# Moving one head's softmax scaling from VectorE to GpSimd, and one PSUM copy ahead of a normalisation, in a fused attention and expert kernel

## The chip, the cores and the metric

The kernel runs on one core of one Trainium2 chip. The metric is device time in microseconds (us) of one execution of the whole program, as the median of several runs. Five engines work from queues of their own: PE (TensorE, matmuls; its weight loads are shown as PEld), DVE (VectorE), ACT (ScalarE), POOL (GpSimd) and SP, which only issues DMAs here. They meet at semaphores.

## The reference, cut to what matters

```python
h = concat([patches(x) @ W.T + b, txt], axis=1)             # 8 sequences of 36 + 512 tokens, width 192
h = h + attn(layernorm(h)); h = h + experts(layernorm(h))

def attn(x):                                                # 3 heads of 64
    scores = einsum('blhe,bmhe->bhlm', q, k) / 8
    scores = scores * where(m >= l, gamma_h ** (m - l), 0)  # zeroed, not masked out
    w = softmax(scores, axis=-1)
    o = einsum('bhlm,bmhe->blhe', w, v)
    o = (o - mean(o)) / sqrt(var(o) + eps)                  # per sequence and head
    return (o.reshape(B, L, D) * gn_weight + gn_bias) @ Wo.T

def experts(x):                                             # 16 experts, 8 chosen per token
    return sum(comb[:, e] * (gelu(x @ w1[e]) @ w2[e]) for e in range(16))
```

A key before the query has the score zero, so it still counts in the softmax: every row of probabilities has a stored part on and above the diagonal and one common value for all keys below it, whose sums over the values come in through 4 extra columns.

## The kernel before, in words

The work has two parts. The first 315 us or so are attention, one sequence b at a time, eight in all (b = 0, 1, a hardware loop over 2 to 6, and 7). Each of the functions called `body` gives one engine its order for one sequence. The second part is the experts: 24 weight tiles for each of 9 token tiles, PE-dense, which the change does not touch.

A sequence's 548 queries are cut into five blocks I = 0 to 4 (four of 128, one of 36). The stored scores of block I have 580, 452, 324, 196 and 68 columns, 1620 in all. One head of one sequence runs like this:

- PE makes the scores in PSUM (`scores`). DVE multiplies them by the decay and takes row maxima (`apply_decay`, the custom instruction of L912), then negates the maxima (`nm`, L918: one column after block 0, four columns at the end).
- ACT takes the exponentials with row sums (`exps`, L598), block by block, into `pr0` (heads 0 and 2) or `pr1` (head 1), and the exponential of the zero score (L595).
- DVE makes the denominators: three small instructions (L925, L927, L929). It then scales the five blocks of `pr` by them (L935). Together these are `normalise`. It starts with a wait for all five exponentials of that head (`exp_done`), and ends with the semaphore `probs_ready`. For head 2 ACT does two of the five blocks (L565).
- PE transposes `pr` in four groups of 4, 4, 4 and 3 blocks (`probs_transpose`, L1316). It waits for the scaling before the first. ACT copies each group from PSUM to `pt` (`pt_copy`, L516). PE multiplies by the values (`attend`), six products, of which the first three need the groups 0 and 1, the fourth the group 2, the last two the group 3. Each shows as two rows per product in the trace.

Between these lie other pieces. On PE: `values` makes the value rows after head 1's scores; its last block waits until DVE has done all decays of head 1. `gn_sums` is a 4-column product on DVE's statistics of the previous sequence's output (`gn_partial`, L943 to L950). On DVE: `norm_stats` for the next sequence in front of head 1's decay, `gn_partial` between the two `normalise` calls, and `gn_variance` (L954 to L960) behind the second. On POOL, one sequence at a time: `rstd_of` (power, L425, and two small ones, L426 and L428), `halve_w1` (two casts L447 and two subtractions L450 of 384 columns), `gn_coefficients` (L459 to L465), which ends with `y_coeff`, and a small copy (L434). On ACT: `v_copy` between head 1's exponentials, and `y_round` and `y_whole` (L626), which scale the previous sequence's output and wait for `y_coeff`.

In the last sequence (b = 7) ACT also normalises the first expert tile (`second_norm(0)`) ahead of head 0's exponentials, and DVE splits that tile's transposes (`x2_rest`) behind head 1's decay; PE's first router products (`logits(0, 2)`, L1178 with `rw`) wait for these.

Of the kernel before, what the change touches and what calls it, by code (L numbers as in the profile page):

```python
# [38 lines left out]
NT = -(-L // P)  # L39
# [58 lines left out]
def nth(b, per, k):  # L98

    return b * per + k  # L100


def early_fusion(nc, patches, txt, tok_w, tok_b, gammas, gn_w, gn_b, attn_w, w1, w2, out):
# [9 lines left out]
    with ctx:  # L113
# [112 lines left out]
        s_done, decayed, nm_ready = sem("s_done"), sem("decayed"), sem("nm_ready")  # L226
        exp_done, den_ready, probs_ready = sem("exp_done"), sem("den_ready"), sem("probs_ready")
        probs_scaled = sem("probs_scaled")
        pt_done, pt_copied = sem("pt_done"), sem("pt_copied")
# [168 lines left out]
        def _(pool):  # L398
# [57 lines left out]
            def gn_coefficients(t):  # L456
# [8 lines left out]
                pool.tensor_tensor(gshift[:, :], gnb[:, :], gsub[:, :], ALU.subtract).then_inc(y_coeff, 1)  # L465

            def second_rstd(t):
                rstd_of(t, ln2_var, rstdb, mvb, vepsb, nmrb, ln2_rstd, SEG)
# [17 lines left out]
            def body(b, tail, later, more):  # L486
                if not more:
                    second_rstd(0)
                    second_twice(0)
                if more:  # L490
                    rstd_of(b + 1, ln1_var, rstd, mv, veps, nmr, ln1_rstd)
                halve_w1(b)
                if tail:
                    gn_coefficients(b - 1)
                if more:
                    twice(ln1_normed, nth(b, 1, 1), xn, xn_ready)
# [15 lines left out]
        def _(sc_eng):  # L512
# [141 lines left out]
            def body(b, tail, later, more):  # L654
# [27 lines left out]
                else:  # L682
                    logits_exp(0)
                if tail:
                    y_round(t, 0)
                pt_copy(b, 1, (0, 1))
                if tail:
                    y_whole(t, 0)
                    y_round(t, 1)
# [101 lines left out]
        def _(dve):  # L791
# [127 lines left out]

            def normalise(b, hh):  # L920

# [7 lines left out]
                last = dve.reciprocal(inv_den[s][:, :], den[s][:, :])  # L929
                if hh == 2:  # L930
                    last.then_inc(den_ready, 1)
                dve.drain()
# [104 lines left out]
            def body(b, tail, later, more):  # L1037
# [10 lines left out]
                if more:  # L1048
                    norm_stats(b + 1, st6, mv, veps, ln1_var)
                apply_decay(b, 1)  # L1050
                if not more:
                    x2_rest(0, 0, 4)
                    x2_rest(0, 1, 5)
                normalise(b, 0)
                if tail:
# [120 lines left out]
        def _(pe):  # L1176
# [133 lines left out]
            def probs_transpose(b, hh, groups=(0, 1, 2, 3)):  # L1310
# [7 lines left out]
                for g in groups:  # L1318
                    if g == 0:

                        pe.wait_ge(probs_ready, nth(b, H, hh + 1))
                        if hh == 2:
# [270 lines left out]
```

## Time and profile before

| | |
|---|---|
| median of 3 runs | 849.03 us (848.9 to 854.23) |
| the profiled execution | 850.09 us |
| its span in the trace | 848.3 us |
| mean granted TensorE clock | 0.983 of full speed |
| PE busy | 805.3 us, 95% of the span |
| DVE busy | 558.7 us, 66% |
| ACT busy | 508.2 us, 60% |
| POOL busy | 101.1 us, 12% |

Times in the rows are counted from the start of the span. A row in order of time gives its start, the time from its start to the end of its last instruction, the engine, the line in the kernel, the operation, output and inputs, and how many instructions it merges; brackets hold the time for which the engine had stood idle and who released it. Back-to-back instructions of an engine overlap a little, so a row can start shortly before the one ahead of it ends. Each iteration of the loop over sequences takes about 36 us and shows the same pattern; the rows are mostly of b = 2, from about 101 to 137 us.

### The profile page before, as it was taken

What the parts mean: (1) busy time and instruction counts of PE and PEld (TensorE: products, weight loads), DVE (VectorE), ACT (ScalarE), POOL (GpSimd) and SP (SyncE); (2) the same over time, 40 slices, a digit from 0 to 9 for tenths busy, and PEclk for the clock granted to TensorE, in tenths of its full rate; (3) what the DMA queues carried; (4) which work ended last, traced back from release to release, by engine and by line L of the source; (5) the groups of instructions that cost most, each with busy time, mean ns of one, the idle gap of its engine ahead of it and who ended that gap; (6) DMA issues with size and microseconds to landing.
All of it is one profiled execution on the core that took longest, in us unless ns stands there. A gap on an engine that the chain in (4) does not pass through costs nothing.

```text
span 848.3 us, 13687 instructions
## 1 busy us (share of the span) xinstructions
PE 805.3 (95%) x4336; PEld 678.4 (80%) x4336; DVE 558.7 (66%) x1559; ACT 508.2 (60%) x1134; POOL 101.1 (12%) x187
## 2 busy tenths in 40 slices
PE   6799999999999998799999999999999999999997
PEld 2677878797787876677888888888888888888886
DVE  5667677677767777565666666666666566666654
ACT  1367867778777774465555645556555556465443
POOL 2022020220202208300101001001010010000000
PEclk9689999999999999999999999999999999999999
DMA  7400010101103027213422324134133241241420
GB/s 221 152 19 17 5 40 0 38 0 38 38 0 93 1 60 208 79 50 93 120 63 71 106 62 133 41 85 123 53 96 91 68 128 47 80 96 61 113 56 18
DMA packets 44376, 60.77 MB, mean 72 GB/s; under 512 B 4018, under 2 KB 37762, under 8 KB 44322
## 3 DMA queue, kind: packets, MB, share of 16 engines
q1 hardware_dynamic: 44322, 60.10, 25.5%
q8 instruction: 27, 0.44, 0.2%
q14 instruction: 27, 0.22, 0.1%
HBM read 52.04 MB, written 8.05 MB: 71 GB/s over the span
## 4 chain that ended last, share of the span: by engine, by line
PE 61%; issue 26%; POOL 6%; POOLq 3%; DVE 2%; ACT 2%; DVEq 0%; ACTq 0%
PE ps L1178 58%; POOL w_lo L450 2%; POOLq L427 1%; POOL w_lo L482 1%; PE ps L1378 1%; POOLq L460 1%; POOLq L481 1%; POOL w_r L480 0%; PE ps L1316 0%; PE ps L1487 0%; ACT pt L516 0%; PE ps L1488 0%; DVE sc L912 0%; POOLq L448 0%; PE ps L1397 0%
## 5 line engine op out<-in xcount | busy, mean ns | idle before, releaser
L1089 DVE TENSOR_TENSOR act<-act,gate 128x480 f32<-128x480 f32 (+1 forms) x216 | 145.1, 672 | 120.0 <-ACT act L714 118.7
L1178 PE MATMUL ps<-x,w_hi 128*128 128x480 f32 (+1 forms) x648 | 217.4, 390 | 0.0
L714 ACT ACTIVATE act<-ps 128x480 f32<-128x480 f32 (+1 forms) x216 | 124.0, 574 | 125.9 <-PE ps L1178 125.7
L1178 PE MATMUL ps<-x,w_lo 128*128 128x480 f32 (+1 forms) x432 | 165.6, 383 | 0.0
L867 DVE TENSOR_TENSOR act_lo<-act,act_hi 128x480 fp32r<-128x480 f32 (+1 forms) x216 | 144.3, 668 | 0.1
L1178 PEld LDWEIGHTS ps<-x,w_hi 128*128 128x128 f32 x648 | 122.5, 189 | 19.8
L516 ACT ACTIVATE act_hi<-act 128x480 fp32r<-128x480 f32 (+1 forms) x216 | 130.8, 605 | 7.9 <-DVE act L1089 7.9
L1178 PEld LDWEIGHTS ps<-x,w_lo 128*128 128x128 f32 x432 | 81.8, 189 | 13.3
L1178 PE MATMUL ps<-act_hi,w_hi 128*128 128x480 f32 (+1 forms) x216 | 83.9, 388 | 6.6 <-DVE act_lo L867 6.6
L1178 PE MATMUL ps<-act_lo,w_hi 128*128 128x480 f32 (+1 forms) x216 | 83.8, 388 | 0.0
L1178 PE MATMUL ps<-act_lo,w_r 128*128 128x480 f32 (+1 forms) x216 | 83.0, 384 | 0.0
L1178 PE MATMUL ps<-act_hi,w_lo 128*128 128x480 f32 (+1 forms) x216 | 82.8, 384 | 0.0
L1178 PE MATMUL ps<-pt,v 68*128 68x512 f32 (+5 forms) x288 | 82.4, 436 | 0.0
L1178 PE MATMUL ps<-act_hi,w_r 128*128 128x480 f32 (+1 forms) x216 | 82.3, 381 | 0.0
L1178 PEld LDWEIGHTS ps<-pt,v 128*128 128x128 f32 (+1 forms) x288 | 49.0, 190 | 31.1 <-issue 21.6
L598 ACT ACTIVATE pr<-sc,nm 128x580 f32<-128x580 f32 (+4 forms) x120 | 66.8, 559 | 10.7 <-DVE nm L918 10.7
L912 DVE CUSTOM_DVE_ANT_0 sc<-ps,decay 128x548 f32<-128x548 f32 (+4 forms) x120 | 49.7, 458 | 35.5 <-PE ps L1178 33.3
L516 ACT ACTIVATE pt<-ps 128x384 f32<-128x384 f32 (+3 forms) x120 | 48.4, 466 | 23.8 <-PE ps L1316 23.6
L1316 PE MATMUL ps<-ident,pr 128*128 128x128 f32 (+1 forms) x360 | 47.2, 276 | 11.6 <-DVE pr L935 9.1
L425 POOL TENSOR_TENSOR rstdb<-vepsb,neg_half 128x4 f32<-128x4 f32 x9 | 12.2, 1353 | 364.9 <-DVE vepsb L989 364.9
L1178 PEld LDWEIGHTS ps<-act_hi,w_hi 128*128 128x128 f32 x216 | 40.5, 187 | 16.4 <-DVE act_lo L867 9.9
L1316 PEld LDWEIGHTS ps<-ident,pr 128*128 128x128 f32 (+1 forms) x360 | 39.1, 132 | 15.7 <-DVE pr L935 10.9
(173 smaller groups left out, 1318.1 us busy)
## 6 DMA issues: line engine op xcount, KB each, us to landing
gate<-comb_dram SPq DMA_DIRECT2D x112, 240.0 KB, 3.3
gate<-comb_dram SPq DMA_DIRECT2D x32, 256.0 KB, 3.7
w_raw<-w SPq DMA_DIRECT2D x16, 384.0 KB, 3.9
h_dram<-h SPq DMA_DIRECT2D x8, 384.0 KB
res<-h_dram SPq DMA_DIRECT2D x7, 360.0 KB, 4.5
out<-res SPq DMA_DIRECT2D x7, 360.0 KB, 3.2
h<-txt SPq DMA_DIRECT2D x3, 672.0 KB
decay_rows<-drow SPq DMA_DIRECT2D x1, 1014.0 KB, 8.0
```

The lines of the kernel that those rows point to most:

```text
L425: pool.tensor_tensor(rs[:, :], ve[:, :], neg_half[:, 0:n], ALU.pow)
L427: pool.drain()
L450: last = pool.tensor_tensor(w1_lo[:, c, cols], w1_raw[:, c, :], w1_hi[:, c, cols], ALU.subtract)
L460: pool.drain()
L516: return a.activation(dst, src, ACT.Copy)
L598: last = a.activation(pr[s][:r, cols], sc[s][:r, cols], ACT.Exp, bias=nm[s][:r, I:I + 1], accum_out=row_sum[s][:r, I:I + 1])
L714: a.activation(act[j % 3][:, 0:n], ps[:, up_bank(j), 0:n], ACT.Gelu_apprx_tanh).then_inc(gelu_done, 1)
L867: return dve.tensor_tensor(dst, src, hi, ALU.subtract)
L912: dve.tensor_tensor_reduce(out=dst, in0=src, in1=tab, scale=1.0 / 8, scalar=0.0 if I else NEG, op0=ALU.mult, op1=ALU.max, accum_out=mx[s][ ...
L1089: dve.tensor_tensor(act[j % 3][:, 0:n], act[j % 3][:, 0:n], gate[e % 4][:, 0:n], ALU.mult).then_inc(gated, 1)
L1178: return pe.matmul(dst, w, x, start=start, stop=stop)
L1316: return pe.transpose(dst, pr[s][:, at:at + n], ident[:, :])
```

## The change

For head 0 the scaling is taken from DVE. DVE makes head 0's denominators ahead of head 1's decay (`denominators(b, 0)`) and signals `first_den`; POOL waits for it, scales the five blocks of `pr0` (`normalise_first`), and signals `first_probs`, for which PE waits in place of `probs_ready`. On POOL this is ahead of `rstd_of` and `halve_w1`; in b = 7 behind `second_twice`. On ACT the copies of head 1's first two groups of transposes go ahead of `y_round`.

```diff
+            def normalise_first(b):
+
+                pool.wait_ge(first_den, nth(b, 1, 1))
+                apart(pool, "pool")
+                for I in range(NT):
+                    t = pr[0][:rows(I), OFF[I]:OFF[I] + WIDTH[I]]
+                    last = pool.tensor_scalar(t, t, inv_den[0][:rows(I), I:I + 1], None, ALU.mult)
+                last.then_inc(first_probs, 1)
...
                 if not more:
                     second_rstd(0)
                     second_twice(0)
+                normalise_first(b)
                 if more:
                     rstd_of(b + 1, ln1_var, rstd, mv, veps, nmr, ln1_rstd)
                 halve_w1(b)
...
+                pt_copy(b, 1, (0, 1))
                 if tail:
                     y_round(t, 0)
-                pt_copy(b, 1, (0, 1))
-                if tail:
                     y_whole(t, 0)
                     y_round(t, 1)
                 pt_copy(b, 1, (2, 3))
...
-            def normalise(b, hh):
+            def denominators(b, hh):
...
                 last = dve.reciprocal(inv_den[s][:, :], den[s][:, :])
-                if hh == 2:
-                    last.then_inc(den_ready, 1)
+                if hh != 1:
+                    last.then_inc((first_den, None, den_ready)[hh], 1)
+
+            def normalise(b, hh):
+                s = hh % 2
+                denominators(b, hh)
                 dve.drain()
...
                 if more:
                     norm_stats(b + 1, st6, mv, veps, ln1_var)
+                denominators(b, 0)
                 apply_decay(b, 1)
                 if not more:
                     x2_rest(0, 0, 4)
                     x2_rest(0, 1, 5)
-                normalise(b, 0)
                 if tail:
                     gn_partial(t)
                 normalise(b, 1)
...
-                        pe.wait_ge(probs_ready, nth(b, H, hh + 1))
+                        if hh:
+                            pe.wait_ge(probs_ready, nth(b, 2, hh))
+                        else:
+                            pe.wait_ge(first_probs, nth(b, 1, 1))
```

DVE's queue in the loop body before, from the end of `norm_stats` over head 1's decay to the statistics of the previous sequence's output (`st`, `mv`, `veps`: the next sequence's statistics; `sc`, `mx`, `nm`: scores, maxima, negated maxima; `gst`: the output's statistics):

```order
L828 TENSOR_SCALAR veps<-mv 128x5
...
L912 ISA sc,mx<-ps,decay 128x548
...
L918 TENSOR_SCALAR nm<-mx 128x4
L923 ISA
L925 TENSOR_TENSOR den<-zero_score,lower_count 128x5
L927 TENSOR_TENSOR den<-den,row_sum 128x5
L929 RECIPROCAL inv_den<-den 128x5
L935 TENSOR_SCALAR pr<-pr,inv_den 128x580
...
L943 BN_STATS gst<-ot 128x6 x2
```

There the denominators stand behind the decay. The same stretch of DVE's queue in the changed kernel:

```order
L838 TENSOR_SCALAR veps<-mv 128x5
L933 ISA
L935 TENSOR_TENSOR den<-zero_score,lower_count 128x5
L937 TENSOR_TENSOR den<-den,row_sum 128x5
L939 RECIPROCAL inv_den<-den 128x5
...
L922 ISA sc,mx<-ps,decay 128x548
...
L928 TENSOR_SCALAR nm<-mx 128x4
L955 ISA
L957 BN_STATS gst<-ot 128x6 x2
```

The three denominator instructions moved in front of the decay, and the five scalings are gone from the queue.

POOL's queue in the loop body of the changed kernel, from its start to the split of w1 (before, the body began with the `rstd` row):

```order
L474 TENSOR_SCALAR pr<-pr,inv_den 128x580
L474 TENSOR_SCALAR pr<-pr,inv_den 128x452
L474 TENSOR_SCALAR pr<-pr,inv_den 128x324
L474 TENSOR_SCALAR pr<-pr,inv_den 128x196
L474 TENSOR_SCALAR pr<-pr,inv_den 36x68
...
L426 TENSOR_TENSOR rstd<-veps,neg_half 128x5
...
L448 COPY w_hi<-w_raw 128x384
...
L451 TENSOR_TENSOR w_lo<-w_raw,w_hi 128x384
```

Everything that POOL did for a sequence is now queued behind the five scalings and behind their wait.

ACT's queue in the loop body before, behind the normalisation of the next sequence (`xn`; `y` and `ot` with `gshift` are `y_round` and `y_whole`, `pt` the copies of transposes):

```order
L546 ACTIVATE xn<-h,nmr,rstd 36x192
L626 ACTIVATE y<-ot,gshift,gscale 128x548
...
L516 ACTIVATE pt<-ps 68x512
...
L516 ACTIVATE pt<-ps 128x384
L626 ACTIVATE ot<-ot,gshift,gscale 128x548
```

Here `y_round` stands first. The same stretch of ACT's queue in the changed kernel:

```order
L557 ACTIVATE xn<-h,nmr,rstd 36x192
...
L527 ACTIVATE pt<-ps 68x512
...
L527 ACTIVATE pt<-ps 128x384
L637 ACTIVATE y<-ot,gshift,gscale 128x548
L637 ACTIVATE ot<-ot,gshift,gscale 128x548
```

The three copies of the groups 0 and 1 changed places with the first of the four instructions that wait for `y_coeff`.

## Rows read from the trace of the kernel before

**Rows 1.** The page: busy us, share of the span, instructions.

```profile
PE 805.3 (95%) x4336; PEld 678.4 (80%) x4336; DVE 558.7 (66%) x1559; ACT 508.2 (60%) x1134; POOL 101.1 (12%) x187
```

**Rows 2.** Waits of PE: who was waited for, us in total, times, longest.

```profile
PE ps L1316 <- DVE pr L935: 9.1, 7, 1.4
...
PE ps L1178 <- DVE gmv L950: 3.3, 7, 0.5
```

**Rows 3.** PE in order of time, b = 0 and then b = 2.

```profile
50.34 1.83 PE L1316 MATMUL ps<-ident,pr 128*68 128x128 f32 x15 [1.37 <-DVE pr L935]
...
120.64 1.83 PE L1316 MATMUL ps<-ident,pr 128*68 128x128 f32 x15 [1.37 <-DVE pr L935]
122.95 0.36 PE L1178 MATMUL ps<-gmv,head_mean 128*128 128x4 f32 x2 [0.47 <-DVE gmv L950]
123.31 3.50 PE L1178 MATMUL ps<-pt,v 68*128 68x512 f32 x12
126.64 1.04 PE L1316 MATMUL ps<-ident,pr 128*68 128x128 f32 x8
...
129.91 3.40 PE L1178 MATMUL ps<-pt,v 68*128 68x512 f32 x12
```

**Rows 4.** DVE in order of time, b = 2.

```profile
114.95 0.73 DVE L912 CUSTOM_DVE_ANT_0 sc<-ps,decay 128x548 f32<-128x548 f32 x1 [1.63 <-PE ps L1178]
...
117.48 0.89 DVE L918 TENSOR_SCALAR nm<-mx 128x4 f32<-128x4 f32 x1
118.28 0.15 DVE L925 TENSOR_TENSOR den<-zero_score,lower_count 128x5 f32<-128x5 f32 x1
...
119.02 1.57 DVE L935 TENSOR_SCALAR pr<-pr,inv_den 128x580 f32<-128x580 f32 x5
...
123.50 1.57 DVE L935 TENSOR_SCALAR pr<-pr,inv_den 128x580 f32<-128x580 f32 x5
```

**Rows 5.** ACT in order of time, b = 2.

```profile
113.89 0.19 ACT L598 ACTIVATION_READ_ACCUMULATOR pr<-sc,nm 36x1 f32 x1
...
117.53 0.66 ACT L516 ACTIVATE v<-ps 128x128 f32<-128x128 f32 x2 [0.69 <-PE ps L1178]
118.40 0.21 ACT L595 ACTIVATE zero_score<-nm 128x5 f32<-128x5 f32 x1 [0.21 <-DVE nm L918]
...
121.31 1.06 ACT L516 ACTIVATE pt<-ps 68x512 f32<-68x512 f32 x3 [0.20 <-PE ps L1316]
...
127.68 0.84 ACT L626 ACTIVATE y<-ot,gshift,gscale 128x548 fp32r<-128x548 f32 x1 [1.94 <-POOL gshift L465]
128.43 1.04 ACT L516 ACTIVATE pt<-ps 68x512 f32<-68x512 f32 x3
...
130.83 0.96 ACT L516 ACTIVATE pt<-ps 128x512 f32<-128x512 f32 x2
```

**Rows 6.** Groups on POOL, shapes kept apart: busy us, mean ns of one; idle before.

```profile
L450 POOL TENSOR_TENSOR w_lo<-w_raw,w_hi 128x384 f32 x10 | 9.9, 1014 | 1.1 <-issue 1.1
L425 POOL TENSOR_TENSOR rstd<-veps,neg_half 128x5 f32<-128x5 f32 x8 | 9.4, 1181 | 162.9 <-DVE veps L828 162.9
...
L447 POOL CAST w_hi<-w_raw 128x384 f32 x10 | 4.8, 506 | 0.4
```

**Rows 7.** POOL in order of time, b = 2.

```profile
116.35 1.98 POOL L450 TENSOR_TENSOR w_lo<-w_raw,w_hi 128x384 f32 x2 [0.23 <-issue]
```

**Rows 8.** DVE in order of time, b = 7.

```profile
294.69 0.73 DVE L912 CUSTOM_DVE_ANT_0 sc<-ps,decay 128x548 f32<-128x548 f32 x1 [2.68 <-PE ps L1178]
...
298.66 0.17 DVE L925 TENSOR_TENSOR den<-zero_score,lower_count 128x5 f32<-128x5 f32 x1
```

**Rows 9.** ACT in order of time, b = 7: the end of head 0's exponentials.

```profile
295.52 0.19 ACT L598 ACTIVATION_READ_ACCUMULATOR pr<-sc,nm 36x1 f32 x1
```

**Rows 10.** PE in order of time, b = 7: router products, and head 1's third group.

```profile
299.66 1.41 PE L1178 MATMUL ps<-rw,x 128*128 128x32 f32 x12
...
309.93 1.01 PE L1316 MATMUL ps<-ident,pr 128*128 128x128 f32 x7 [0.62 <-ACT pt L516]
```

More of the change, by code:

```diff
@@ L227, in early_fusion @@
         exp_done, den_ready, probs_ready = sem("exp_done"), sem("den_ready"), sem("probs_ready")
+        first_den, first_probs = sem("first_den"), sem("first_probs")
         probs_scaled = sem("probs_scaled")
```

## The prediction, made before the changed kernel ran

> **What bounds the kernel now.** I read the page first: PE is busy for 95% of the span [rows 1], so only PE's gaps are to be had. The view of PE's waits names them. Two kinds repeat once per sequence: 9.1 us in 7 waits of the head transposes (L1316) for DVE's scaled `pr`, and 3.3 us in 7 waits for DVE's `gmv` [rows 2]. Then the engines in order of time, for one sequence, b = 2, whose pattern repeats.
>
> PE would begin head 0's transposes at 120.64 - 1.37 = 119.27, right behind the value rows, and begins at 120.64 [rows 3]. DVE's five scalings run from 119.02 to 120.59 [rows 4] and PE starts 0.05 us later; that is the hand-off I use below. They come so late only because of DVE's order: head 0's exponentials were over at 113.89 + 0.19 = 114.08 [rows 5], and the whole decay of head 1, 114.95 to 118.3, stood in between [rows 4]. The second wait, 0.47 us, is the same lateness passed on: DVE reaches the output's statistics behind the scalings. PE starts `gn_sums` at 122.95 and the first product with the values at 123.31 [rows 3].
>
> **The denominators in front of the decay.** From the first small instruction to the first scaling DVE takes 119.02 - 118.28 = 0.74 us [rows 4]. Started 0.05 us behind the exponentials, they run from 114.13 to 114.87. DVE stood idle for 1.63 us before 114.95, waiting for PE's scores [rows 4], so they fill a hole. Head 1's decay starts 0 to 0.4 us late (the 0.4 if a semaphore between the small ones stalls). What is queued behind is the decay and its `nm`, for which ACT waits; ACT's second exponential of head 1 stands behind a value copy that waits for PE until 117.53 [rows 5], which hides that much. No cost in the loop.
>
> **The scaling on POOL.** No row shows POOL's `tensor_scalar` with a column of factors. The bounds: a cast of 384 columns takes 506 ns, a subtraction of two inputs 1014 ns [rows 6]. For 1620 columns, 4.22 times as much, that is 2.13 or 4.28 us. I take 2.13 us as the nearer row: the product streams one tensor, like the cast. POOL starts at 114.9 and ends at 117.05, or 119.2 by the other row. Both are before 119.27, so PE's 1.37 us goes either way in the loop. Gone from DVE are 1.57 + 0.74 us between the decay and the statistics, so `gmv` comes some 2 us earlier and the 0.47 us goes too. PE's own floor for the first product with the values is then 123.31 - 1.37 - 0.47 = 121.47.
>
> **What is late next: ACT.** The product also needs the copies of groups 0 and 1. They stand at 121.31 behind a run of exponentials and value copies that began at 118.40, with only 0.20 us of waiting in it [rows 5]. So the copies start 118.40 to 121.31 less 0.20 = 2.71 us behind that start, take 1.06, and hand over in 0.05: 3.82 us in all. Can the start at 118.40 move? ACT waited there for `nm`, a 4-column instruction that took 0.89 us on DVE [rows 4] and ended at 118.37, just as POOL's subtractions ended, 116.35 + 1.98 = 118.33 [rows 7]. I read this as DVE held by POOL. If POOL is between long operations at 117.5 in the changed kernel, ACT starts when the value copies let it, 117.53 + 0.66 less an overlap of 0.1 = 118.1, and the product at 121.9: 1.4 us gained. If POOL holds `nm` as before, it starts at 118.4 and the product at 122.2: 1.1 us gained. With POOL's products over at 117.05, next in its queue is the power (1181 ns for 5 columns [rows 6], hardly any data), so the first is possible. I take the middle, 1.25 us, and keep both ends.
>
> The page "GPSIMD Engine Reference" of the Trainium skill, section "Key points", says that GpSimd shares its SBUF interfaces with VectorE, in contention with VectorE's instructions in a 2-port mode or with two SBUF inputs. The 0.89 us agree. By that rule alone a POOL product still running at 117.5 would hold `nm`, and the gain would be the 1.1 us.
>
> **Does the gain survive to the next sequence?** Three places behind it.
> - Head 1's scalings on DVE began at 123.50, 1.13 us behind the end of the copies (121.31 + 1.06). Now: copies end at 121.9, scalings 123.0 to 124.6. PE wants them at 126.64 - 1.4 = 125.2 [rows 3, 4]. Margin 0.6.
> - `y_coeff`: ACT's `y` began at 127.68, 2.61 us behind the end of head 1's scalings (125.07); now 127.2. Before, 127.68 to 130.83 held three `y` instructions and the copies of groups 0 and 1 (about 0.93 us as spaced), so three `y` take 2.22 us. With the copies ahead of them the group 2 copy starts at 127.2 + 2.2 = 129.4 and is done near 129.9. PE begins head 1's products at 129.91 - 1.4 = 128.5 and needs group 2 after 932 of their 1828 columns, 1.73 us of the 3.40 [rows 3, 5]: 130.2. Margin 0.3. In the old order the first copies would start at 127.2 + 0.75 and PE's third group would wait for them about 0.8 us; this is what the ACT edit is for, it gains nothing by itself in the loop.
> - POOL's queue: the power and two small ones, the casts and the subtractions now start at 117.05 and take some 4.9 us (1.8 + 1.0 + 2.0 and gaps), to about 122. The subtractions end before head 1's denominators at 122.3. Margin 0.3. The next sequence's `rstd` is wanted by ACT only at about 123.
>
> **The eight sequences.** b = 2 to 6: 5 x 1.25 = 6.25 us. b = 1: its wait for `pr` is 9.1 - 6 x 1.36 = 0.9 to 1.0 us, the shortest of the seven [rows 2]; I take 1.0. b = 0: there is no `gmv` wait and, at the start, no hole in DVE's time, so I let the 0.74 us of denominators count against the 1.37 us [rows 3]: 0.7 (bounds 0 and 1.37). b = 7: there head 0's exponentials end only at 295.52 + 0.19 = 295.71 [rows 9], a microsecond after head 1's decay began at 294.69 [rows 8]. DVE now waits for them: decay at 295.71 + 0.05 + 0.74 = 296.5, 1.8 us late. From the decay's start to the end of the two `x2_rest` DVE takes 298.66 - 294.69 = 3.97 us [rows 8], so they are done at 300.4 and PE's router products start there instead of at 299.66 [rows 10]: 0.8 us lost. The `gmv` wait (0.47) vanishes behind it, so some 0.35 is left at the first product; and head 1's third group, which waited 0.62 us for ACT's copy [rows 10], has it earlier by the ACT edit. I put b = 7 at 0, between -0.5 (gain) and +0.8.
>
> Sum: 6.25 + 1.0 + 0.7 + 0 = 7.95, say 8.0 us. The expert part is untouched and shifts as a whole. Profiled execution: 850.09 - 8.0 = 842.1. The median of the runs shown lies 1.06 us under it, so the forecast is 849.03 - 8.0 = **841.0 us**. With both ends of every term it goes from 5 x 1.1 + 0.9 + 0 - 0.8 = 5.6 to 5 x 1.4 + 1.0 + 1.4 + 0.5 = 9.9: 839.1 to 843.4.
>
> **Rivals.**
> *POOL is slow and in the way (about 847).* If the scaling runs at the subtraction's rate, POOL is done with it at 119.2 and with the split of w1 near 124.1, right through DVE's head-1 denominators and scalings (123.0 to 124.6). By the 0.89 us row each of these can be held for up to one POOL instruction of 1.0 us. One microsecond there passes to `y_coeff` and to PE's third group, whose margin is 0.3; 0.3 us per sequence is left, 2 us in all. For it: the same collision is in the trace. Against it: one input tensor, not two. The page "Perfetto Trace Analysis" of the Trainium skill, section "Optimizing Scalar/DVE Operations", says just this, that moving work between VectorE and GpSimd might not help because they share an SBUF port; by it nothing much is gained.
>
> *ACT does keep up (about 837).* If the copies were no limit, PE would start at its floor: 1.84 us for each of b = 2 to 6, 1.5 for b = 1, 1.37 for b = 0: 12.1 us. Against it stands the full ACT run of rows 5; it would need ACT to start 0.4 us before its value rows are there.
>
> *Slower: POOL's products become the wait (about 858).* Before, the scaled head 0 was there at 120.59; POOL, starting at 114.9, is later than that if it needs over 5.7 us, 3.5 ns a column. Each microsecond above costs PE one in every sequence, and in b = 7 as well. At 7 us, 4.3 ns a column, 1.3 x 7 = 9.1 us are added to 849.03. For it: no row shows the operation. Against it: its slowest neighbour needs 2.6 ns a column with two inputs.
>
> **How the numbers follow.** Forecast 0.61, slow POOL 0.23, ACT keeps up 0.10, POOL the wait 0.06. A measurement of this kernel can tell about 1% from no change, 8.5 us, so 840.5 is the border. About half of the forecast's band lies below it: 0.30, with the 0.10 of the second rival 0.40 faster. Slower by that much needs the last rival at nearly its full price: 0.05. The rest, 0.55, is within 1%. The range, 838.5 to 847.5, holds the forecast's band and most of the first rival's.
>
> **What would show it.** Right: PE's waits for `pr` and `gmv` in head 0 gone, and in their place one of 0.4 to 0.8 us per sequence in front of the products with the values, released by ACT's `pt`; POOL's five scalings near 2.1 us from first to last; the `nm` of head 1 short again; in b = 7 DVE's decay 1.8 us behind its old place relative to PE's scores, and a PE wait for `x2_rest`. Wrong: a wait of L1330 for POOL in the loop; `nm` or head 1's scalings stretched by POOL; a PE wait for `pt` in front of head 1's third or fifth product.

## The result, and the profile after

| | before | changed |
|---|---|---|
| median of 20 runs each | 850.92 us | 856.57 us |
| lowest and highest | 848.62, 855.54 us | 853.12, 858.27 us |
| ratio, with its 95% interval | | 1.0045, 1.0028 to 1.0061 |
| the profiled execution, its span | 850.09, 848.3 us | 857.33, 855.6 us |

The change makes the kernel slower, by the ratio above 0.45%. The forecast was 841.0 us with a range of 838.5 to 847.5, so it had the wrong sign. Each kernel's times fall in two groups (848.6 to 850.3 and 851.5 to 855.5 us before; 853.1 to 854.9 and 856.5 to 858.3 us after), and group by group the medians rose by 4.5 and 3.4 us. The profiled executions differ by more, 7.2 us.

The page of the changed kernel shows where work went: POOL has 43.5 us more than in [rows 1], DVE only 3.3 us less, though head 0's five scalings, 1.57 us a sequence [rows 4], have left it.

```profile
PE 808.4 (94%) x4336; PEld 679.5 (79%) x4336; DVE 555.4 (65%) x1519; ACT 508.4 (59%) x1134; POOL 144.6 (17%) x227
```

The waits of PE in the changed kernel: who was waited for, us in total, times, longest.

```profile
PE ps L1330 <- POOL pr L474: 9.4, 7, 2.4
...
PE ps L1330 <- DVE pr L949: 5.1, 6, 0.9
PE ps L1192 <- ACT pt L527: 2.0, 6, 0.3
PE ps L1192 <- DVE mx L922: 1.9, 1, 1.9
```

The 9.1 us for DVE's `pr` of [rows 2] have become 9.4 us for POOL's, and the 3.3 us for `gmv` are gone. Two new kinds came: the scaling of head 1, and ACT's copies, six times each.

POOL's groups, shapes kept apart: busy us, mean ns of one; idle before.

```profile
L474 POOL TENSOR_SCALAR pr<-pr,inv_den 128x580 f32<-128x580 f32 x8 | 13.9, 1744 | 159.2 <-DVE inv_den L939 159.2
...
L474 POOL TENSOR_SCALAR pr<-pr,inv_den 128x452 f32<-128x452 f32 x8 | 11.3, 1415 | 0.0
...
L474 POOL TENSOR_SCALAR pr<-pr,inv_den 128x324 f32<-128x324 f32 x8 | 8.7, 1094 | 0.0
L474 POOL TENSOR_SCALAR pr<-pr,inv_den 128x196 f32<-128x196 f32 x8 | 6.2, 772 | 0.0
...
L474 POOL TENSOR_SCALAR pr<-pr,inv_den 36x68 f32<-36x68 f32 x8 | 3.6, 445 | 0.0
```

A column costs (1744 - 445) / (580 - 68) = 2.54 ns, and each instruction about 0.27 us besides: 5.4 us for the five (5.38 from first to last in the row below), 2.5 times what I took (2.13) and 26% over the bound that I called the upper one (4.28).

Now one sequence of the changed kernel, b = 2, in order of time. PE:

```profile
125.13 1.83 PE L1330 MATMUL ps<-ident,pr 128*68 128x128 f32 x15 [1.17 <-POOL pr L474]
126.80 0.28 PE L1192 MATMUL ps<-gmv,head_mean 128*128 128x4 f32 x2
126.94 3.48 PE L1192 MATMUL ps<-pt,v 68*128 68x512 f32 x12
131.26 1.04 PE L1330 MATMUL ps<-ident,pr 128*68 128x128 f32 x8 [0.83 <-DVE pr L949]
...
133.54 0.98 PE L1330 MATMUL ps<-ident,pr 128*128 128x128 f32 x7
134.36 1.89 PE L1192 MATMUL ps<-pt,v 68*128 68x512 f32 x6
136.58 1.67 PE L1192 MATMUL ps<-pt,v 128*128 128x512 f32 x5 [0.33 <-ACT pt L527]
```

POOL, over the same time:

```profile
119.70 5.38 POOL L474 TENSOR_SCALAR pr<-pr,inv_den 128x580 f32<-128x580 f32 x5 [21.92 <-DVE inv_den L939]
125.04 1.19 POOL L426 TENSOR_TENSOR rstd<-veps,neg_half 128x5 f32<-128x5 f32 x1
...
126.83 0.96 POOL L448 CAST w_hi<-w_raw 128x384 f32 x2
128.00 2.17 POOL L451 TENSOR_TENSOR w_lo<-w_raw,w_hi 128x384 f32 x2 [0.21 <-issue]
131.98 0.70 POOL L460 TENSOR_TENSOR grstd<-gvar,neg_half 128x2 f32<-128x2 f32 x1 [1.81 <-DVE gvar L974]
```

And DVE:

```profile
119.67 0.73 DVE L922 CUSTOM_DVE_ANT_0 sc<-ps,decay 128x548 f32<-128x548 f32 x1 [0.18 <-PE ps L1192]
...
122.19 0.17 DVE L928 TENSOR_SCALAR nm<-mx 128x4 f32<-128x4 f32 x1
...
124.23 0.16 DVE L962 TENSOR_TENSOR gtmp<-gmv 128x2 f32<-128x2 f32 x1
...
127.45 0.35 DVE L937 TENSOR_TENSOR den<-den,row_sum 128x5 f32<-128x5 f32 x1
...
128.14 2.97 DVE L949 TENSOR_SCALAR pr<-pr,inv_den 128x580 f32<-128x580 f32 x5
```

Three things are to be read here. POOL ends head 0's scaling at 119.70 + 5.38 = 125.08, PE begins 0.05 us later and had waited 1.17 us: POOL has taken DVE's place in [rows 3], almost at the old price. Secondly, everything on POOL came late behind it, and its subtractions, 128.00 to 130.17, now lie upon head 1's scalings on DVE: five instructions that took 1.57 us before [rows 4] take 2.97 us, and PE waits 0.83 us for them. Thirdly, `y` on ACT and the copies behind it slip too, and the last products wait 0.33 us. The last row of POOL says why `y` is late: POOL stood idle for 1.81 us before `grstd`, the first step to `y_coeff`, until DVE had made `gvar` behind its stretched scalings. It was the held DVE that made `y` late, not the length of POOL's queue.

To count the loss I use marks: the first transposes that PE makes of each sequence, those of the normalised input `xn` (not those of `pr`). For b = 2 this is, in the kernel before,

```profile
97.19 1.26 PE L1216 MATMUL ps<-ident,xn 128*128 128x128 f32 x10
```

and in the changed one

```profile
101.88 1.25 PE L1230 MATMUL ps<-ident,xn 128*128 128x128 f32 x10
```

From one mark to the next it is 35.95 us in the loop before and 36.31 us after (five sequences, +1.8 us); b = 1 has 35.32 and 35.58 (+0.26); b = 0 has 35.25 and 39.75 (+4.5); from b = 7's mark to the transposes of `xn` for the expert tile behind it +0.75. That is 7.3 us, the difference of the spans. These spans are of one execution each, and most of the 4.5 us of b = 0 goes with the place of a low clock and not with the new order, as the end of the next section shows. Against the forecast (8.0 us less) 8.05 us are missing in the loop, 1.3 in b = 1, 5.2 in b = 0 and 0.75 in b = 7.

### The profile page after: what moved, and what is told of

Read it like the earlier page. It is cut to its first block, busy times and chain, and to the rows that moved or that the text cites. A ratio compares the mean times of both kernels' runs of the same rounds, so it can differ in the third digit from the quotient of the medians.

```text
span 855.6 us, 13676 instructions
## 1 busy us (share of the span) xinstructions
PE 808.4 (94%) x4336; PEld 679.5 (79%) x4336; DVE 555.4 (65%) x1519; ACT 508.4 (59%) x1134; POOL 144.6 (17%) x227
## 3 DMA queue, kind: packets, MB, share of 16 engines
q1 hardware_dynamic: 44322, 60.10, 25.1%
HBM read 52.04 MB, written 8.05 MB: 70 GB/s over the span
## 4 chain that ended last, share of the span: by engine, by line
PE 73%; POOL 9%; issue 6%; ACT 5%; POOLq 5%; DVE 2%; DVEq 0%; ACTq 0%
PE ps L1192 67%; POOL pr L474 3%; PE ps L1330 3%; ACT pr L609 2%; POOLq L428 2%; POOL w_lo L451 2%; POOL w_lo L492 1%; PE ps L1230 1%; ACT pt L527 1%; POOL rstd L426 1%; PE ps L1395 1%; ACT y L637 1%; POOLq L449 1%; POOLq L461 1%; POOLq L491 1%
## 5 line engine op out<-in xcount | busy, mean ns | idle before, releaser
L1192 PE MATMUL ps<-pt,v 68*128 68x512 f32 (+5 forms) x288 | 86.7, 449 | 2.0 <-ACT pt L527 2.0
L474 POOL TENSOR_SCALAR pr<-pr,inv_den 128x580 f32<-128x580 f32 (+4 forms) x40 | 43.0, 1094 | 159.2 <-DVE inv_den L939 159.2
L1330 PE MATMUL ps<-ident,pr 128*128 128x128 f32 (+1 forms) x360 | 50.0, 287 | 15.4 <-POOL pr L474 9.4
L1330 PEld LDWEIGHTS ps<-ident,pr 128*128 128x128 f32 (+1 forms) x360 | 41.3, 138 | 19.3 <-POOL pr L474 11.4
```

What stands on the lines that cost most here:

```text
L474: last = pool.tensor_scalar(t, t, inv_den[0][:rows(I), I:I + 1], None, ALU.mult)
L1192: return pe.matmul(dst, w, x, start=start, stop=stop)
L1330: return pe.transpose(dst, pr[s][:, at:at + n], ident[:, :])
```

## The experiments

My theory after the result: POOL's scaling runs at 2.54 ns a column, and this one wrong size does it all, by PE's wait for it and by what it pushes behind it on POOL. The rivals: that the denominators in front of the decay cost something, that ACT's new order does, or that the forecast of the rest (gain 1.25 us, then ACT the limit) was wrong too. The first four kernels take the change apart. All kernels of this section were run once, except the three for which a median of four is given; one kernel's total varies by some 4 us from run to run, so the argument rests on the rows and on the distances from mark to mark.

**Without ACT's edit.**

```diff
+                if tail:
+                    y_round(t, 0)
                 pt_copy(b, 1, (0, 1))
                 if tail:
-                    y_round(t, 0)
                     y_whole(t, 0)
```

> The changed kernel with ACT's old order. The first copies of head 1 stand behind y_round again, whose coefficients now come about 1 us after the transposes they copy. Theory (the ACT edit is needed because POOL's queue is late): PE's third group of head 1 waits 1 to 1.6 us and the loop period of 36.31 us rises to 37.3 to 37.9, the total by 7 to 10 us. Rival (the ACT edit does nothing where the bound is POOL's scaling): period stays within 0.1 of 36.31.

Measured 862.84 us (before, on the same chip, 849.18), and 37.3 us from mark to mark in the loop, except for b = 4 with 39.0, where PE's clock was granted at half from 209 to 212 us, behind such a wait for ACT. PE in order of time, b = 2, of this kernel:

```profile
122.34 1.83 PE L1331 MATMUL ps<-ident,pr 128*68 128x128 f32 x15 [1.16 <-POOL pr L474]
...
128.46 1.04 PE L1331 MATMUL ps<-ident,pr 128*68 128x128 f32 x8 [0.83 <-DVE pr L950]
...
132.31 1.01 PE L1331 MATMUL ps<-ident,pr 128*128 128x128 f32 x7 [1.40 <-ACT pt L527]
```

A third wait joins the other two: ACT stands in front of `y`, late with `y_coeff`, and head 1's third group waits 1.40 us for the copies behind it. So the ACT edit is not what costs; with the late POOL it saves 1.0 us a sequence.

**ACT's edit alone**, in the kernel before.

```diff
-                if tail:
-                    y_round(t, 0)
                 pt_copy(b, 1, (0, 1))
                 if tail:
+                    y_round(t, 0)
                     y_whole(t, 0)
```

> The kernel before with the ACT edit alone. PE has no wait for copies in the loop, so the period stays at 35.96 us within 0.1; the waits of 0.37 (b = 1) and 0.62 us (b = 7) in front of head 1's third group go. Total 0.5 to 1.5 us under before. Rival (the copies now delay y and with it the next statistics): period above 36.1.

Measured 848.60 us, and in the loop 35.66 us from mark to mark instead of 35.95. That is 0.29 us a sequence which the theory had at nothing. (The total met the expectation only because b = 0 took 37.24 us instead of 35.25, by its clock; see below.) The place shows by distances: from head 1's first transposes to its third group it is 2.57 us in the kernel before (b = 3 to 6) and 2.29 us here. PE was losing 0.28 us there all along, which the move of ACT's copies took back, and no idle bracket in [rows 3] says so.

**The denominators early, alone**: DVE still scales, behind the decay.

```diff
+                denominators(b, 0)
                 apply_decay(b, 1)
...
-                normalise(b, 0)
+                scale(b, 0)
```

> The kernel before with head 0's denominators in front of head 1's decay, the scaling left on DVE behind it. Theory (the move fills a hole of DVE): scaling starts 0.65 us earlier, PE's wait for pr falls from 1.37 to about 0.7 us and the period from 35.96 to 35.2 to 35.4; in b = 7 some 0.5 to 1 us are lost. Total 2 to 4 us under before. Rival (waiting for the exponentials holds the decay up in the loop too): period 35.9 or more.

Measured 853.19 us, more and not less than before, yet in the loop 35.59 to 35.64 us from mark to mark, 0.35 less than before. PE's wait for `pr` falls from 1.37 to 0.66 us, and 0.52 us of ACT's `pt` appears in front of head 1's third group, where this kernel has the old ACT order. So in the loop the early denominators cost nothing, as I had said. The loss is in b = 0, which takes 39.56 us (4.3 more than before) and is looked at below, and behind b = 7's mark, from where the rest takes 1.3 us more.

**POOL scales only the last block** (68 of 1620 columns), the rest of the change as it is. Four blocks stay unscaled, so the output is wrong, and the kernel serves only to measure.

```diff
-                for I in range(NT):
+                for I in range(NT - 1, NT):
```

> The changed kernel with POOL scaling only the smallest of head 0's five blocks; four blocks of head 0's probabilities stay unscaled. This stands for a POOL that is fast enough. Theory (everything lost is POOL's slow scaling and what it pushes behind it): PE's waits for pr and gmv are gone, a wait for ACT's copies of 0.4 to 0.8 us takes their place, as forecast, and the period is 34.5 to 34.9 us. If ACT keeps up: 34.1. Rival (the loss lies in the denominators' place or in the queue of POOL whatever its length): period 35.5 or more.

Measured 841.86 us (before 849.18). PE in order of time, b = 2:

```profile
119.87 1.80 PE L1330 MATMUL ps<-ident,pr 128*68 128x128 f32 x15
...
122.56 3.50 PE L1192 MATMUL ps<-pt,v 68*128 68x512 f32 x12 [0.68 <-ACT pt L527]
...
125.90 1.04 PE L1330 MATMUL ps<-ident,pr 128*68 128x128 f32 x8
...
128.19 0.98 PE L1330 MATMUL ps<-ident,pr 128*128 128x128 f32 x7
```

This is the kernel that I had forecast: no wait for `pr` or `gmv`, in their place 0.68 us for ACT's copies, and the first product with the values 1.35 us earlier after the mark than before (24.62 instead of 25.97, b = 3 to 6). With the hidden 0.28 us a sequence is 1.63 us shorter, 34.32, which is less than the 34.5 to 34.9 that I expected. For the loop the rivals fall. Against this kernel the changed one loses 1.98 us a sequence, and the marks split them: 0.43 to the first product (POOL late), 0.98 more to head 1's first transposes (DVE held), 0.57 behind its last products (`y` late).

The next kernels ask which part of the 1.98 us is the place in POOL's queue, and which the scaling itself.

**The split of w1 last on POOL.** Nothing on POOL is made faster.

```diff
                 normalise_first(b)
                 if more:
                     rstd_of(b + 1, ln1_var, rstd, mv, veps, nmr, ln1_rstd)
-                halve_w1(b)
                 if tail:
                     gn_coefficients(b - 1)
                 if more:
                     twice(ln1_normed, nth(b, 1, 1), xn, xn_ready)
+                halve_w1(b)
```

> The changed kernel with POOL's split of w1 moved from in front of gn_coefficients to the end of POOL's body. Theory (of the 1.98 us that the period of 36.31 lies above that of the one-block kernel, 34.32, 0.43 is POOL's late scaling and 1.55 is POOL's w1 subtractions holding DVE's head-1 denominators and scalings, passed on to y and PE): head 1's five scalings on DVE are 1.57 us again instead of 2.97, PE's waits of 0.83 for pr and 0.33 for pt go, the period is 34.7 to 35.0. Rival (DVE is late because it waits for ACT and POOL's scaling, not for the w1 split): period 36.0 or more.

Measured 847.66 us, which by itself says little: before, seven runs on the same chip gave a median of 853.6 and went from 848.18 to 854.3. PE, then DVE, in order of time, b = 2:

```profile
123.34 1.83 PE L1330 MATMUL ps<-ident,pr 128*68 128x128 f32 x15 [1.17 <-POOL pr L474]
...
128.46 1.04 PE L1330 MATMUL ps<-ident,pr 128*68 128x128 f32 x8
```

```profile
126.17 1.57 DVE L949 TENSOR_SCALAR pr<-pr,inv_den 128x580 f32<-128x580 f32 x5
```

The wait for POOL is the same 1.17 us, but DVE's scalings are back at 1.57 us, and from mark to mark it is 34.74 us, 1.57 less than in the changed kernel. So the collision with the subtractions, and the late `y` that comes of it, were worth 1.57 us, POOL's lateness by itself 0.4. The larger loss was the place of work that nothing waits for. That POOL's subtractions held DVE's scalings is shown by this: neither was altered, they were only moved apart.

**Two blocks on POOL** (1032 of 1620 columns), three on DVE behind the decay, w1's split where the change has it.

```diff
-                for I in range(NT):
+                for I in range(2):
...
+                scale(b, 0)
                 if tail:
                     gn_partial(t)
```

> The changed kernel with POOL scaling only the blocks 0 and 1 of head 0 (1032 of 1620 columns) and DVE the three small ones behind head 1's decay; the queue order of POOL is the changed kernel's. Everything is computed. Theory: POOL is done 3.1 us after first_den, before PE wants it, and the w1 split ends 2.2 us earlier, near DVE's head-1 denominators: period 34.4 to 35.2, total 7 to 12 us under the changed kernel. Rival (any product on POOL in this place costs more than it saves): period 35.96 or more.

Measured 844.53 us, 35.15 us from mark to mark. No wait for `pr` is left, but 0.39 us for `gmv` and 0.39 us for ACT's copies in front of the last products. A smaller load on POOL clears part of the way, yet `y` is still late.

**Both together, and b = 0 and b = 7 in the old order**: two blocks on POOL for b = 1 to 6, w1's split last, and in the first and last sequence the denominators and all five scalings on DVE behind the decay.

```diff
-                normalise_first(b)
+                if not isinstance(b, int) or b == 1:
+                    normalise_first(b)
...
-                denominators(b, 0)
+                early = not isinstance(b, int) or b == 1
+                if early:
+                    denominators(b, 0)
                 apply_decay(b, 1)
```

> As two_blocks, with the w1 split at the end of POOL's body, and in b = 0 and b = 7 the kernel before's way: denominators behind head 1's decay, all of head 0 scaled by DVE. Everything is computed. Theory (both collisions gone, and no early wait where head 0's exponentials are late): period 34.3 to 34.6, b = 0 and b = 7 as before, so the total is 8 to 10 us under before and 12 to 15 under the changed kernel. Rival (the late w1 split collides with y_rest and head 2's work instead): period above 35.

Measured 839.55 us, median of four (838.91 to 842.94), against 853.6, median of seven; lowest against lowest it is 9.3 us less. The ratio is 0.9865, interval 0.9812 to 0.9917. From mark to mark 34.31 us, the distance of the kernel that hardly scaled at all, and here everything is computed. This version beats both kernels.

**What is slow on POOL?** The five instructions were given four forms: a constant factor, a tensor by itself, a copy, and the old form.

```diff
-                    last = pool.tensor_scalar(t, t, inv_den[0][:rows(I), I:I + 1], None, ALU.mult)
+                    if I == 0:
+                        pool.tensor_scalar(t, t, 0.5, None, ALU.mult)
+                    elif I == 1:
+                        pool.tensor_tensor(t, t, t, ALU.mult)
+                    elif I == 2:
+                        pool.tensor_copy(t, t)
+                    else:
+                        last = pool.tensor_scalar(t, t, inv_den[0][:rows(I), I:I + 1], None, ALU.mult)
```

> A measurement of POOL's forms on head 0's blocks: block 0 times a constant, block 1 times itself (two tensor inputs), block 2 copied onto itself, blocks 3 and 4 as in the change; so head 0's probabilities are wrong in blocks 0 to 2. The change's rows are 1744, 1415, 1094, 772 and 445 ns, that is 2.54 ns per column and 0.27 us. Theory (the column of factors makes it slow): block 0 in 0.7 to 0.9 us, block 2 in 0.45, block 1 in about 1.2 (2.6 ns per column as the subtractions). Rival (tensor_scalar is slow whatever the factor): block 0 in 1.74 us.

POOL's groups, shapes kept apart:

```profile
L475 POOL TENSOR_SCALAR pr<-pr 128x580 f32<-128x580 f32 x8 | 13.4, 1669 | 156.6 <-DVE inv_den L946 156.6
...
L477 POOL TENSOR_TENSOR pr<-pr 128x452 f32<-128x452 f32 x8 | 7.5, 942 | 0.0
...
L481 POOL TENSOR_SCALAR pr<-pr,inv_den 128x196 f32<-128x196 f32 x8 | 6.2, 772 | 0.0
...
L479 POOL COPY pr<-pr 128x324 f32<-128x324 f32 x8 | 3.7, 463 | 0.0
```

Measured 850.0 us. A constant factor saves 4% (1669 instead of 1744 ns for 580 columns): not the column of factors is slow but `tensor_scalar`. The product of two tensors takes 942 ns where `tensor_scalar` took 1415, and the copy of 324 columns 463 ns where it took 1094. My picture "one input streams like the cast" was wrong for this operation.

**So the same product as tensor by tensor**, with the factor repeated along the row.

```diff
-                    last = pool.tensor_scalar(t, t, inv_den[0][:rows(I), I:I + 1], None, ALU.mult)
+                    factor = inv_den[0][:rows(I), I:I + 1].broadcast_to([rows(I), WIDTH[I]])
+                    last = pool.tensor_tensor(t, t, factor, ALU.mult)
```

> The changed kernel with POOL's scaling written as a product of two tensors, the factor broadcast along the row, in place of tensor_scalar. By the four-forms run a product of 452 columns takes 0.94 us against 1.42. Theory (the form is what cost): the five take 3.3 to 3.6 us instead of 5.38, POOL is done before PE's value rows are over, so PE's wait for POOL's pr in the loop is gone; the w1 subtractions still meet DVE's head-1 work, though 1.9 us earlier, so the period is 34.6 to 35.5. Rival (broadcast factors stream as slowly as tensor_scalar, 2.5 ns a column): 5 us or more and a period near 36.3.

Measured 845.87 us (before, seven runs on the same chip: median 851.82, 849.15 to 855.12). POOL's groups for the two largest blocks:

```profile
L475 POOL TENSOR_TENSOR pr<-pr,inv_den 128x580 f32<-128x580 f32 x8 | 9.2, 1155 | 157.5 <-DVE inv_den L940 157.5
L475 POOL TENSOR_TENSOR pr<-pr,inv_den 128x452 f32<-128x452 f32 x8 | 7.5, 942 | 0.0
```

PE in order of time, b = 2:

```profile
119.07 1.80 PE L1331 MATMUL ps<-ident,pr 128*68 128x128 f32 x15
...
121.77 3.50 PE L1193 MATMUL ps<-pt,v 68*128 68x512 f32 x12 [0.78 <-ACT pt L528]
```

The five instructions take 1155 + 942 + 728 + 515 + 295 = 3635 ns, 1.68 ns a column, a third less for the same product. PE no longer waits for POOL anywhere. It is 35.15 us from mark to mark, as with two blocks: the first product has its forecast place, and 0.25 and 0.57 us are lost behind it. The subtractions, from 121.32 to 123.28 us, now lie upon head 1's denominators on DVE: the first two of the three take 0.27 and 0.89 us, where they took 0.17 each in the changed kernel's head 0.

**The changed kernel, with b = 0 and b = 7 in the old order**, as above but with five blocks on POOL and the w1 split where the change has it.

```diff
-                normalise_first(b)
+                if not isinstance(b, int) or b == 1:
+                    normalise_first(b)
```

> The changed kernel with b = 0 and b = 7 in the kernel before's way (denominators behind the decay, DVE scales head 0). Theory (of the 7 us between the two profiled spans the loop makes 2.1 to 2.4, the rest lies in b = 0 and b = 7, and of b = 0's 4.5 about 3 are the TensorE clock): period still 36.31, b = 0 back at 35 to 37.3 us by the clock it gets, the kernel 1.5 to 3 us slower than before. Rival (the ends cost nothing of their own): as the changed kernel, 4 us or more slower.

Measured 855.54 us, median of four (853.02 to 856.5), ratio 1.0039, interval 1.0003 to 1.0076. It did not take back b = 0: 39.14 us there, although its code for b = 0 is again that of before. So most of the 4.5 us of b = 0 comes without the change's order there, and the expected 1.5 to 3 us over the kernel before became 3.7; the last part of this section has the place of it. Behind b = 7's mark this kernel takes 0.8 us less than the changed one, in one trace of each.

**Everything learnt, with tensor by tensor**: all five blocks on POOL in b = 1 to 6 as tensor by tensor, the w1 split last, and the ends in the old order (the edits shown above, together).

> Product of two tensors on POOL for all five blocks, w1 split at the end of POOL's body, b = 0 and b = 7 as in the kernel before. Everything is computed. Theory: no collision and POOL in time, the period is that of the one-block kernel, 34.3 us, the time within 1 us of the two-blocks kernel's 839.6 in the same TensorE clock. Rival (the longer hold of the port by two-input products delays nm of head 1 and the statistics on DVE): period 34.6 or more.

Measured 843.06 us, median of four (839.62 to 843.26), ratio 0.9888, interval 0.9851 to 0.9924; the profiled execution 839.62. From mark to mark 34.33 us, with one wait of 0.78 us for ACT's copies. Its profiled span, 837.8 us, and that of the two-block version, 837.7, are the same; the medians differ because three of four runs of this one lie near 843 and three of four of the other near 839. Which of the two is better can't be told from these runs.

**Where b = 0 loses its time.** Two kernels with the same code for b = 0 and equal starts lie 3.2 us apart there: the changed one with 39.75 us, and the one without ACT's edit (which acts from b = 1 on) with 36.56. PE in order of time, first in the changed kernel:

```profile
47.50 0.34 PE L1192 MATMUL ps<-aw_hi,xa_hi 128*68 128x256 f32 x1 [1.93 <-DVE mx L922]
...
50.73 3.41 PE L1330 MATMUL ps<-ident,pr 128*68 128x128 f32 x15 [2.43 <-POOL pr L474]
```

then in the one without ACT's edit:

```profile
50.05 1.83 PE L1331 MATMUL ps<-ident,pr 128*68 128x128 f32 x15 [1.64 <-POOL pr L474]
```

The same fifteen transposes take 3.41 and 1.83 us. PE by stretches, in the changed kernel: from:to, length, PE busy (instructions), granted clock, DMA share, GB/s.

```profile
42.00:44.00 2.00, 2.00 (x19) 1.00 0.00 0
44.00:46.00 2.00, 1.57 (x14) 1.00 0.00 0
46.00:48.00 2.00, 0.50 (x4) 1.00 0.00 0
50.00:52.00 2.00, 1.27 (x6) 0.50 0.00 0
52.00:54.00 2.00, 2.00 (x12) 0.50 0.02 4
```

And in the one without ACT's edit:

```profile
42.00:44.00 2.00, 2.00 (x13) 0.50 0.00 0
...
46.00:48.00 2.00, 2.00 (x11) 0.50 0.00 0
50.00:52.00 2.00, 1.91 (x16) 1.00 0.00 0
```

Each has one stretch at 0.50, the 1.2 GHz level, between 36 and 60 us. In the kernel without ACT's edit it lies from about 42 to 48 us, where PE makes value rows and must wait for DVE anyway; the slower products fill that wait. In the changed kernel PE does these at 2.4 GHz, stands idle for 1.93 and 2.43 us, and comes back at 1.2 GHz for the transposes and products up to about 59 us, where nothing hides it. Of the traces, the kernel before, the one without ACT's edit, the four forms and both complete variants with tensor by tensor have it early, and b = 0 takes 34.1 to 36.6 us. The changed kernel, the early denominators alone, w1's split last, and the changed kernel with the old ends have it late and for some 10 us, and b = 0 takes 39.1 to 39.8 us. Four others (ACT's edit alone, one block, and both with two blocks) have it late but for 3 to 8 us (34.6 to 37.2 us). Old and new orders of b = 0 are among the early ones and among the late ones.

## Why the prediction was wrong

**"The scaling on POOL" is the step that failed.** I bounded `tensor_scalar` by a cast and a subtraction (2.13 and 4.28 us), called the second the upper bound, and took the first, "as the nearer row". It took 5.38 us, above both (POOL, b = 2, 119.70 to 125.08). Everything after it was worked out with POOL free at 117.05; by the measured rate, from a start at 114.9, it would have been 120.3, a microsecond behind the 119.27 at which PE wants the block. "PE's 1.37 us goes either way in the loop" fell with it. The Trainium skill, page "GPSIMD Engine Reference", section "4.1 Engine selection", calls one-input elementwise work on GpSimd roughly line-rate, where it sets the engine beside VectorE. The copy (463 ns for 324 columns) comes near VectorE's own `tensor_scalar` (385 ns for as many, the mean of 24 in the kernel before); GpSimd's `tensor_scalar`, 1094 ns for them, does not, and the measurement decides.

**The rivals.** The first, "POOL is slow and in the way", named the right mechanism and place: the w1 split through DVE's head-1 denominators and scalings, and from there to `y_coeff`. I priced it at one microsecond in front of a margin of 0.3, with PE's wait for `pr` gone. In fact 2.97 instead of 1.57 us on DVE, `y` late, and the wait for POOL came together: 1.98 us a sequence, more than the whole gain of 1.63 us that the kernel with one block shows. The third rival, "POOL's products become the wait", had its point at 5.7 us. At 5.38 us POOL was 0.3 us short of it, and indeed the first product is 0.9 us earlier after the mark than before (25.05 and 25.97), not later. What made the kernel slower was the two together, which I had kept apart; their sum had no chance of its own.

**What held.** With the scaling all but taken out, the forecast of the loop stands: the first product 1.35 us earlier against 1.25 (1.1 to 1.4); 0.68 us for ACT's copies against 0.4 to 0.8; the waits for `pr` and `gmv` gone. The denominators filled DVE's hole: the decay stood idle 0.18 us for PE's scores behind them. That the total, 841.86 us, is so near the forecast of 841.0 is luck. Trace against trace the loop gained 8.2 us instead of 6.25, b = 1 1.5 instead of 1.0, and the part behind b = 7's mark 0.8 instead of nothing, while b = 0 lost 1.3 us instead of gaining 0.7 and the start up to b = 0's mark took 1.1 us more.

**"This is what the ACT edit is for, it gains nothing by itself in the loop."** Half right. With it the late `y` cost 1.0 us a sequence less. By itself it gained 0.29 us a sequence, since 0.28 us were lost there before. I had read the missing bracket in front of head 1's third group as no wait.

**"If POOL holds `nm` as before."** My reading of the 0.89 us row was right for a subtraction of two tensors, and the scalings at 2.97 us against 1.57 confirm it. But I let the rule of the Trainium skill on the shared SBUF interfaces (page "GPSIMD Engine Reference", section "Key points") count for any POOL product still running. POOL's scaling ran from 119.70 to 125.08, and the `nm` in the middle of it took 0.17 us. Nor was `gtmp` at 124.23 held, whose 0.16 us are those of the kernel before (0.16 us, the median of eight), and over all 24 `nm` of four columns the mean fell from 343 to 172 ns. No hold shows beside this operation of POOL, and the rows decide.

**b = 0.** Forecast a gain of 0.7 us. DVE's decay moved from 44.01 to 45.09, 1.1 us instead of at most 0.74, because DVE also stood 0.21 us for ACT and had no hole. POOL ended at 50.67, so the transposes began at 50.73 instead of 50.34. That is 0.4 us of loss, by the same wrong size. The kernel without ACT's edit, with the same code there, lost 1.3 us in all against the kernel before; the other 3.2 us are the low clock at another place. I had not looked at the clock row by row, and a term for it was missing: it stood at nothing, without a reason.

**b = 7.** Forecast 0, within -0.5 and +0.8; measured 0.75 us lost, at the edge. The steps of the forecast show: the decay came 1.73 us later after the mark (forecast 1.8), the router products 0.80 us later (0.8). Head 0's transposes began 25.1 us after the mark instead of 24.1, so by then the order had cost 1.0 us; it is 25.0 to 25.7 in every kernel with this order in b = 7, and 24.1 to 24.2 in every one with the old order. Then these transposes took 3.30 us instead of 1.8, beside a granted clock of 0.67 from 307 to 312 us. The kernel before has a stretch at 0.50 too, from 325 to 328 us, so how the clock and the ACT edit make 0.75 of the 1.0 was not separated.

**What stays open.** Why the 1.2 GHz stretch falls early or late in b = 0, and how long it lasts. The order of b = 0 does not decide it, since both orders show both places; whether it shifts the odds can't be told from one trace of each kernel. The two groups of times of the result would fit such a stretch: among the changed kernel's 20 runs the mean granted clock is 0.982 or 0.983 in the 9 of the lower group and 0.976 to 0.980 in the 11 of the upper. Where in the upper ones the low clock lies was not shown. Nor was it tried whether `tensor_scalar` is as slow between two different tiles.

## What to carry to other kernels

Before work is moved to another engine, time that very operation there in the form it will have: rows of other operations did not bound `tensor_scalar` on GpSimd, and the same product written as tensor by tensor took a third less. Then walk down the receiving engine's queue: here work that nobody waited for was pushed against VectorE's instructions and cost 1.57 us a sequence, four times POOL's lateness by itself (0.4 us), and moving it to the end took that back. Where a gap is suspected, compare distances from start to start, since a loss of 0.28 us showed in no idle bracket.

## What the runs showed of the hardware that I had not expected

- On GpSimd, in place and in float32, `tensor_scalar` took 1744 ns for 580 columns (2.54 ns a column) and 1669 with a constant factor. The product of two tensors took 1155 ns for the same 580, with one of them a repeated column (1.68 ns a column), and a copy 463 ns for 324.
- Beside GpSimd's two-tensor subtractions (about 1.0 us each) VectorE's small and one-tensor instructions took longer, up to the end of a subtraction: `nm` 0.89 us [rows 4] instead of 0.17, a 5-column `den` 0.89 instead of 0.17, five scalings 2.97 instead of 1.57 us. GpSimd's `tensor_scalar` did not hold the same `nm` (0.17 us).
- The 1.2 GHz stretch near 50 us costs the same code 3.2 us more or less (39.75 and 36.56 us for b = 0), by whether it lies on work that waits anyway (about 42 to 48 us) or on work behind PE's idle time (about 49 to 59 us).
